# Two-layer transformer block: the steps between the two attention layers in a hand-given order

## The reference, cut to what matters

```python
def _L0_ffn_ref(x, w_gate, w_up, w_down):      # after layer 0's causal attention (8 heads of 128, 2 groups)
    gate = fp4_linear(x, w_gate)               # fp4_linear: x and w quantised to FP4 in blocks of 16,
    y = fp4_linear(x, w_up)                    # then multiplied
    h = jax.nn.silu(gate) * y                  # 352 wide
    return fp4_linear(h, w_down)
def _L1_attn_ref(x, Wq, bq, Wk, bk, Wv, bv, Wo, bo):   # not causal: all 2048 keys for every query
    q = (x @ Wq.T + bq).reshape(b, n, G, hpg, HD)      # 4 groups of 4 heads, 8 values a head
    k = (x @ Wk.T + bk).reshape(b, n, G, HD)
    scores = jnp.einsum('bqghd,bkgd->bghqk', q, k) * scale
    attn = jax.nn.softmax(scores, axis=-1)
x = _layernorm(x + _L0_attn_ref(x, ...))
x = _layernorm(x + _L0_ffn_ref(x, ...))
x = _layernorm(x + _L1_attn_ref(x, ...))
x = _layernorm(x + _L1_ffn_ref(x, ...))               # 8 experts, dense, weighted by a thresholded softmax
```

## Time and profile before

| | |
|---|---|
| median of 3 runs | 1371.78 us |
| the profiled execution | 1369.12 us |
| its span, first to last instruction | 1367.4 us |
| TensorE busy | 1240.4 us |
| VectorE busy | 1057.8 us |
| ScalarE busy | 808.1 us |
| GpSimd busy | 138.0 us |

### The profile page before, as it was taken

How to read it: one execution, slowest core, us unless ns; L and a number is a source line. 1 busy time by engine, 2 the same in 40 slices (tenths; PEclk the granted TensorE clock), 3 DMA queues, 4 the chain that set the end, 5 groups by cost and what they waited for, 6 DMA issues and landing times.

```text
span 1367.4 us, 19101 instructions
## 1 busy us (share of the span) xinstructions
PE 1240.4 (91%) x6326; PEld 546.6 (40%) x6326; DVE 1057.8 (77%) x2263; ACT 808.1 (59%) x1602; POOL 138.0 (10%) x257
## 2 busy tenths in 40 slices
PE   5689989999999974689999999999999999999895
PEld 3345445445443332333333443334443433334333
DVE  4667896798664658588999897999889999999424
ACT  3234435455545431248888766787666787778771
POOL 6110111103010020100000002000012000000030
PEclk8669989999999985679999999999999999999998
DMA  4010100110000000000000000000000000000000
GB/s 107 19 30 17 31 1 1 24 24 1 1 1 9 0 9 0 1 8 9 9 2 9 8 2 16 8 1 9 8 4 14 9 9 1 9 9 1 1 1 16
DMA packets 13794, 15.04 MB, mean 11 GB/s; under 512 B 3864, under 2 KB 8528, under 8 KB 13696
## 3 DMA queue, kind: packets, MB, share of 16 engines
q1 hardware_dynamic: 12720, 13.05, 3.9%
q0 software_dynamic: 976, 0.78, 0.3%
HBM read 3.66 MB, written 1.05 MB: 3 GB/s over the span
## 4 chain that ended last, share of the span: by engine, by line
PE 72%; DVE 16%; issue 5%; ACT 4%; POOL 1%; DMA 1%; SPq 1%; DVEq 0%; POOLq 0%; ACTq 0%
PE ps L876 24%; PE ps L857 15%; PE ps L765 11%; DVE MP L1352 7%; PE ps L853 6%; PE ps L770 4%; ACT PR L1095 2%; PE ps L829 2%; PE ps L794 2%; PE ps L730 1%; DVE ps L1349 1%; PE ps L776 1%; PE ps L761 1%; PE ps L805 1%; DVE ST L1275 1%
## 5 line engine op out<-in xcount | busy, mean ns | idle before, releaser
L1095 ACT ACTIVATE PR<-ps 128x512 f32<-128x512 f32 (+2 forms) x1344 | 697.6, 587 | 372.2 <-PE ps L853 192.7
L1352 DVE TENSOR_REDUCE MP<-ps 128x1 f32<-128x512 f32 x1216 | 763.5, 682 | 118.9 <-PE ps L765 68.2
L876 PE MATMUL ps<-PR,V 128*32 128x512 f32 (+2 forms) x2688 | 431.2, 598 | 2.7 <-ACT OS L970 2.1
L765 PE MATMUL ps<-KO,Q 64*128 64x512 f32 x1024 | 376.1, 460 | 12.6 <-DVE MP L1352 7.5
L857 PE MATMUL ps<-Q,KO 64*128 64x512 f32 x1024 | 331.9, 439 | 11.7 <-DMA Q<-MR 6.1
L857 PEld LDWEIGHTS ps<-Q,KO 64*128 64x128 f32 x1024 | 160.1, 186 | 286.6 <-issue 139.4
L765 PEld LDWEIGHTS ps<-KO,Q 64*128 64x128 f32 x1024 | 167.2, 189 | 91.3 <-ACT PR L1095 38.2
L770 PE MATMUL ps<-KO,QO 96*128 96x512 f32 (+2 forms) x320 | 124.2, 436 | 23.1 <-DVE QO L1333 10.0
L853 PE MATMUL ps<-QO,KO 97*128 97x512 f32 (+3 forms) x320 | 140.7, 453 | 4.5 <-DMA QO<-MR 2.7
L876 PEld LDWEIGHTS ps<-PR,V 128*32 128x32 f32 (+1 forms) x2688 | 74.0, 115 | 126.2 <-issue 67.4
L853 PEld LDWEIGHTS ps<-QO,KO 97*128 97x128 f32 x320 | 61.3, 197 | 131.0 <-issue 81.2
(11 more groups left out here) (211 smaller groups left out, 758.4 us busy)
## 6 DMA issues: line engine op xcount, KB each, us to landing
QO<-Q SPq DMA_DIRECT2D x72, 64.0 KB, 2.0
Q<-QS SPq DMA_DIRECT2D x64, 64.0 KB, 2.0
Q<-MR SPq DMA_DIRECT2D x64, 2.0 KB
result<-V SPq DMA_DIRECT2D x4, 256.0 KB, 2.3
H<-in_L_attn_wq SPq DMA_DIRECT2D x1, 512.0 KB, 3.5
HQT<-in_L_attn_wo SPq DMA_DIRECT2D x1, 512.0 KB, 5.7
ew<-in_L_ffn_expert_w POOLq DMA_DIRECT2D x1, 512.0 KB, 4.5
bq<-in_L_attn_bq POOLq DMA_DIRECT2D x12, 0.1 KB, 3.5
```

The source lines that it names most:

```text
L765: last = nc.tensor.matmul(bank[:, :], Q1[rows, buf, h // 2, q * P:(q + 1) * P], KO1[rows, g, kc * QC:(kc + 1) * QC], start=True, stop=True)
L876: nc.tensor.matmul(dst, VO[layer][:, kt, g, :], PR[:, u % NP_RING, q0:QC], start=kt == 0, stop=kt == key_tiles(layer, c) - 1).then_inc(pv_ ...
L1095: nc.scalar.activation(PR[:, u % NP_RING, q0:QC], ps[:, bank_of_score[u], q0:QC], ACT.Exp, scale=SCALE[layer]).then_inc(exp_done, 1)
L1352: v.tensor_reduce(MP[:, buf, h, q, kc:kc + 1], bank[:, 0:w], AX, ALU.max).then_inc(free, 1)
```

## The change

The even spreading by `interleave` is replaced by `between_layers`, which lists the steps one by one. The 48 early maxima are the same, in the same order, as are all other steps: no instruction is added or removed, and the list before the first step moved and after `k1 3 3` is the same. Of the maxima, 16 now stand before the quantisation of x (5 ahead of `out0`, 3 ahead of `on0`, 5 ahead of `y0`, 3 ahead of `norm0`), 6 behind `xq`, 4 behind `hqT 2`, 2 ahead of `hqT 3`, 6 ahead of `down`, 3 ahead of `norm1`, 4 ahead of `k1 0 3` and 7 behind it. The quantisations have none between their stages. `gate` and `up` stand in pairs: tiles 0 and 1 ahead of the first `quant_h`, tiles 2 and 3 each behind the quantisation of the tile two before. The queries `q1 1 0 1` are moved from ahead of `on0` to behind `norm0`. Of the four key groups of chunk 3 only group 0 stays ahead of the 16 last maxima; groups 1, 2 and 3 and the values stand among them, one after every third step.

```diff
--- before.py
+++ after.py
@@ -15,6 +15,7 @@
 import concourse.bass as bass
 from concourse import mybir
 from contextlib import ExitStack
+from itertools import islice
 
 P = 128
 T = 2048
@@ -431,12 +432,31 @@
                 else:
                     behind = gaps("4", [("on0", 0)]) + (rest0(c - 1) if c else ffn_weights[second:])
 
-            yield from carry + out_copies(outs) + outs
-            beside = queries(1, 0, 1, 1) + maxima(1, 0, 0, 0, [NC - 2]) + maxima(1, 0, 1, 1, range(NC - 2))
-            yield from interleave(attended0(NC - 1) + rest0(NC - 1), beside)
+            yield from between_layers(carry + out_copies(outs), outs)
+
+        def between_layers(carry, outs):
+
+            c, tiles = NC - 1, range(QT)
+            ahead = iter(maxima(1, 0, 0, 0, [NC - 2]) + maxima(1, 0, 1, 1, range(NC - 2)))
+            plain = lambda name, *rest: [step for _, step in quantised(name, *rest)]
+            last = [step for _, step in rest0(c)]
+            keys = [step for step in last if step[0] == "k1"]
+            gates = [[("gate", q), ("up", q)] for q in tiles]
+            yield from carry + list(islice(ahead, 5)) + outs + list(islice(ahead, 3)) + [("on0", 1)]
+            yield from list(islice(ahead, 5)) + [("y0", c)] + list(islice(ahead, 3)) + [("norm0", c)] + queries(1, 0, 1, 1)
+            yield from plain("quant_x", c, 0) + plain("quant_x", c, 1) + [("xq", c)] + list(islice(ahead, 6))
+            yield from gates[0] + gates[1] + plain("quant_h", 0) + gates[2] + [("hqT", 0)] + plain("quant_h", 1)
+            yield from gates[3] + [("hqT", 1)] + plain("quant_h", 2) + [("hqT", 2)] + list(islice(ahead, 4))
+            yield from plain("quant_h", 3) + list(islice(ahead, 2)) + [("hqT", 3)] + list(islice(ahead, 6))
+            yield from [("down", c)] + list(islice(ahead, 3)) + [("norm1", c), ("x2T", c)] + list(islice(ahead, 4))
+            yield from keys[:1] + list(ahead)
 
             work, starts, _ = stream([(1, 0, 0, 0, [NC - 1]), (1, 0, 1, 1, [NC - 2, NC - 1])], False)
-            yield from between(work, -1, starts[1] + BEGUN)
+            others = keys[1:2] + [("v1", c)] + keys[2:]
+            for n, step in enumerate(between(work, -1, starts[1] + BEGUN)):
+                if n % 3 == 2 and others:
+                    yield others.pop(0)
+                yield step
 
         def steps1(c, first, last):
```

## The result

| | before | changed |
|---|---|---|
| median | 1371.32 us (4 runs, 1370.65 to 1372.01) | 1361.74 us (4 runs, 1360.64 to 1362.51) |
| ratio to before | | 0.993, 95% interval 0.9916 to 0.9944 |
| profiled execution | 1369.12 us | 1361.57 us |
| last values of chunk 2 to `row_max` | 490.85 to 591.59: 100.74 us | 490.50 to 583.06: 92.56 us |

A forecast was written before the change was run, and what follows sets the result against it. VectorE's idle time was taken to bound the stretch between layers: 25.3 us of waits less 10.9 remaining less 2.3 extra work gives 12.1 us gain, 1371.8 to 1359.7 us; range 1356.8 to 1365.8.

The forecast's parts named there:

- signs of being wrong: One wait over 4 us at `down`, keys or `y0`; layer 1 of another length; or group 1 maxima waiting for moved queries.
- 2 `y0`: Between `out0` and `norm0`: maxima cover most of TensorE's `on0` and `y0`; VectorE idle 0.5 us, bounds 0 and 1.8.
- 3 `xq`: After quantising x no ready maximum is left, so VectorE waits through the transposes: idle 1.9 us, bounds 1.5 and 1.9.
- 5 `hqT 2`: TensorE has no maxima ahead of these transposes when VectorE finishes quantising: idle 1.7 us, bounds 1.4 and 1.7.
- 7 `down`: TensorE's `down`, 5.1 us at half clock, outlasts the six maxima ahead: VectorE idle 1.5 us, bounds 1.0 and 2.5.
- 8 `x2T`: Three maxima are used up before the norm; VectorE waits for four transposes and a matmul: 1.9 us, bounds 1.5 and 2.0.
- 10 last sixteen: Last maxima with three key groups and values among them; VectorE's lead covers TensorE's excess: idle 0.4 us, bounds 0.3 and 2.5.
- price of not interleaving: 21 maxima no longer alone between quantisation stages cost VectorE 0.11 us more each: 2.3 us more work.
- The overlap of 0.11 us a maximum: On VectorE, a maximum between dependent quantisation stages adds 0.49 us, against 0.60 when bunched, as it starts before the stage ends.
- the waits only moved: Rival: each bunch of maxima runs out one step early, VectorE stays as idle; gain under 2.7 us, about 1371; chance 0.06.
- Half clock: Rival: between the layers TensorE stays at half clock, everything behind comes late; gain 5 to 7 us, about 1366; chance 0.16.
- A cold layer 1: Rival: layer 1's first iteration stays at low clock for longer, ending slower at 1374.7 us; chance 0.03.

The follow-up runs named there:

- the useless matmuls: Changed kernel plus throwaway TensorE matmuls before `xq` (34), the four `hqT` (20, 12, 20, 24) and `x2T` (18): 1357.06 us, ratio 0.9884.
- five of them at `on0`: Changed kernel, three early maxima moved ahead of `xq`, `hqT 2`, `x2T`; throwaway matmuls also before `hqT`, `xq`, `x2T`, `on0` (5), `scores` (9): 1353.21 us.
- The experiment with threes: Kernel before, with maxima standing alone between quantisation stages held back until three are together: 1368.48 us, ratio 0.9979.
- the experiments with ready maxima: Changed kernel with three maxima moved ahead of each of `xq`, `hqT 2`, `x2T`: 1357.19 us; others added throwaway TensorE matmuls, 1351.97 to 1363.43 us.

## Why the prediction was right

I forecast 1359.7 us and a gain of 12.1; it is 1361.7 and 9.6 by the medians, 8.2 in the stretch. The mechanism was right: VectorE's idle time bounds the stretch, what `row_max` gains the end gains, and `row_max` moved forward by 8.2 of the forecast 12.1. None of the signs of being wrong came: the longest wait is 2.0 us, no maximum waits for the moved queries, and what follows the first `scores` takes 772.2 us against 771.2, within the 771 to 776 of all traces. That the medians lie nearer to the forecast (9.6) than the stretch does is not to the prediction's credit: the profiled executions differ by 7.6 us, and executions of the kernel before alone range from 1366.5 to 1373.2. Place by place, in the order of the prediction:

| place | forecast | measured |
|---|---|---|
| 1 start | 2.0 | 1.94 |
| 2 `y0` | 0.5 | 1.56 |
| 3 `xq` | 1.9 | 1.99 |
| 4 gates | 0.2 | 0 |
| 5 `hqT 2` | 1.7 | 1.77 |
| 6 `hqT 3` | 0.5 | 0.45 |
| 7 `down` | 1.5 | 2.02 |
| 8 `x2T` | 1.9 | 1.93 |
| 9 `k1 0 3` | 0.3 | 0.31 |
| 10 last sixteen | 0.4 | 2.37 |
| sum | 10.9 | 14.3 |
| price of not interleaving | 2.3 | 2.7 (10.9 less waiting, 8.2 less stretch) |

Seven places are within 0.2 us. Three are too small, by some 3.5 us together, and TensorE's part of each was priced too low:

- Place 2. I took `y0` at 3.0 us, between the two levels of the clock; it took 3.78 at half clock. The matmuls of the five maxima ahead of it took 1.6 us, not 1.2. In the kernel before, TensorE had no gap from 493.9 to 498.4 us, 1.92 us of it the matmuls of the queries that the change moved away, and its clock rose from 0.5 to 1.00 by the start of `y0`. Whether moving them is what left `y0` at half clock was not tried.
- Place 7. `down` took 4.76 us, less than the 5.1 that I had priced, and the clock did rise at its end as I allowed for (1.00 in its last 0.8 us). But the matmuls of the six maxima ahead of it took 1.67, not 1.3. I had counted 0.43 us a pair, and the earlier trace rows has 0.79 for one alone and 1.22 for four: the first pair costs 0.79.
- Place 10. The same slip is in the 0.65 us for three maxima. A key group and three maxima took TensorE 3.15 us (568.61 to 571.76), not 0.65 + 1.8, against VectorE's 1.8: an excess of 1.3 in place of 0.6. And TensorE did not have the lead that was to absorb it. It had waited itself, 0.56 us until ScalarE had read the keys of group 0 out of their bank and 0.84 until GpSimd had finished them; VectorE's waits then grew to 1.20. How much the excess and how much the lost lead did is not separated.

That half clock is what makes these steps longer than their cover is shown by the useless matmuls: with them places 7 and 10 cost 0.2 us each, and with five of them at `on0` place 2 costs nothing. In place 10 half clock was in the forecast, so there it is a cause of the wait but not of the error.

The overlap of 0.11 us a maximum held. From the first to the last stage the two halves of `quant_x` and the four `quant_h` took 34.65 us before, with 21 maxima among them, and take 24.30 now without: 0.49 us a maximum against 0.60, a price of 2.3 us as forecast. The other 0.4 of the 2.7 lies elsewhere, 0.2 of it in the normalisation behind `y0` (1.34 us against 1.11). The experiment with threes has about 1.0 for some 12 maxima. Without the term the forecast would have been 14.4 against 8.2. The section of the Trainium skill that I weighed ("VectorE: DVE Perf Modes", "The DRAIN you can't avoid") says that the next instruction waits until the pipe is empty, but it goes on to say that one which is not held starts earlier, and the prediction left that out. The trace agrees with this second part: the independent maximum starts 0.08 us before the stage in front of it ends.

The moved queries cost no wait, as forecast, but only because no maximum of group 1 stood ahead of `xq`: the experiments with ready maxima there put one behind their DMA. The rivals: the waits only moved at `xq`, `hqT 2` and `x2T`, not in sum. Half clock was stronger than forecast, but the gain stayed above that rival's 5 to 7 us. A cold layer 1 did not come.

## What to carry to other kernels

Where one engine bounds a stretch of dependent steps, list its waits with their ends and walk the new order place by place with the latencies of the old trace; that gave seven of ten places to 0.2 us. Independent work covers a hand-over only if it stands ahead of the step that the other engine waits for, not behind it in that engine's queue. And price TensorE's steps at the granted clock that the new order is likely to give, not the old one: `y0` went from full to half clock, 2.02 to 3.78 us, by a move of the steps ahead of it, and here the clock alone, with no real work changed, was worth 7 us of 92.

## What was not expected of the hardware

Work that is thrown away made the kernel faster: 128 useless matmuls raise TensorE's clock from 0.65 to 0.92 of full and shorten the stretch by 7.1 us. Where they outlast the wait they cost more than they give (a wait of 5.35 us at `xq`).

The same first part of the program takes from 485.2 to 492.2 us in different executions. Where it took 485.4 the granted clock was 0.97 from 80 to 120 us and 0.99 from 120 to 200, where it took 490.85 it was 0.86 and 0.96, with the same instructions. The clock is not all of it: the three that took 492.2 had 1.00 and 0.82 in the first two 40 us, where the one with 490.85 had 0.79 and 0.67. So a comparison of total times of this kernel under 2 us says little; the same list within the stretch repeated to 0.03 us in one pair and to 0.13 in three kernels.
